# A three-stage convolution kernel: patches in row order, the projection's bias folded into the second group norm, and single matmul blocks between the transposes

## The chip, the cores and the metric

The kernel runs on one core of one Trainium2 chip. The time is the device time of one execution in microseconds (us). A core has TensorE (PE, matmuls and transposes; PEld is its weight load), VectorE (DVE), ScalarE (ACT), GpSimd (POOL), and SyncE (SP), whose queue starts most transfers here. Each engine takes its own instructions in order and waits for the others by semaphores.

## The reference, cut to what matters

The input x has 384 channels of 192 x 192 pixels. Two layers run one behind the other, each behind a group norm over 32 groups:

```python
x = x + conv0(group_norm(x))          # layer 0
x = x + conv1(group_norm(x))          # layer 1

# conv0, its end (channel attention before it, on the image at half size)
out = gelu(attention(q, k, v))                       # (384, 96, 96)
out = repeat(repeat(out, 2, axis=2), 2, axis=3)      # (384, 192, 192)
out = einsum('bchw,oc->bohw', out, w_proj) + b_proj[None, :, None, None]

# conv1: a depthwise 13 x 13, a depthwise 3 x 3 and the identity, each with a batch norm, summed
```

The projection is 1 x 1, so the kernel applies it before the repeat, and each value of the result goes to 2 x 2 pixels.

## The kernel before

Channels lie on partitions, in `CB` = 3 blocks of 128. The stages run one behind the other, with a barrier between them: statistics of x, the QKV stage, the attention matrix, the **Project stage** (`stage_project`), the group norm's constants (`group_affine` with the tag g1), the depthwise kernels (`stage_kernels`), and the **Depthwise stage**.

The Project stage makes the first layer's sum x1 = x + projection and cuts it into patches for the depthwise convolution. It takes 8 image rows (4 at half size) in a step, `STEPS` = 24 steps and a last one that only empties. The work of a step t is written out by hand in `ORDER`, a list that TensorE and ScalarE follow alike:

- **A0 to A2**: TensorE multiplies v by the attention matrix into the bank `pr_ab` (7 matmuls of 384 columns in all, L1019), and ScalarE applies GELU into `ge` (L934).
- **Y0 to Y2**: TensorE projects block n with three matmuls into `pr_yb` (L1028). Then ScalarE adds the bias in place (L937, semaphore `y_ready`), and VectorE adds x (L954, `add`) into the buffer `x1`, writes statistics with `bn_stats` (L959, `record`), and signals `x1_done`.
- **T0 to T11**: the sum of the step before is transposed patch by patch on TensorE (L1005, 39 patches of 128 pixels, up to 4 in a T, two banks `pr_tb`), and ScalarE copies each bank into `turned` (L922). T0 to T3 are block 0, T4 to T7 block 1, T8 to T11 block 2; T3, T7 and T11 hold one patch. A T on TensorE waits until the T two before it is copied (`tr_out`).

A patch is 16 pixels wide and 8 high, shifted by `PAD` = 6 in both directions, so 13 patches (`TJ`) lie across. `x1` holds a patch in column order: `[TJ, TW, TH]`, the row index inside. A step's 8 rows cross the patch edge, so `add` writes 2 rows into the buffer at hand and 6 into the next.

SP stores `turned` to `patch_scratch` for each block (L889, 832 KB) once its four T's are copied, and then loads v (L818, 576 KB) and x (L819, 2304 KB) for the step after next, once `att_done` and `x1_done` of this step are complete. ScalarE's first copy of a block (T0, T4, T8) waits until that block's store of the step before has landed (`stored`).

In the Depthwise stage each partition is one pixel of a patch. TensorE multiplies by a Toeplitz matrix (`cv_toep`) that is loaded for each channel from `toeplitz_scratch` (L1220, 384 KB), row by row in the order of the patch's pixels.

## Time and profile before

| | before |
|---|---|
| time, median of 3 runs | 3220.83 us (3219.31 to 3222.27) |
| time of the profiled execution | 3220.84 us |
| its span in the trace | 3219.1 us |
| PE / DVE / ACT busy over the whole span | 86% / 76% / 43% |
| first matmul of the Project stage | 1747.7 us |
| last copy of the Project stage begins | 2183.65 us |
| first matmul of the Depthwise stage on the chain that ends last | 2252.27 us |

The span runs from the first to the last instruction, and the time lies 1.7 us above it. The chain that ended last is in TensorE for nearly all of the Depthwise stage. The Project stage takes about an eighth of the span.

### The profile page before, as it was taken

How to read it: one execution, taken by the hardware profiler on the slowest of the kernel's cores; microseconds unless marked ns; L12 is line 12 of the kernel's file. 1: busy time of each engine (PE TensorE's matmuls, PEld its weight loads, DVE VectorE, ACT ScalarE, POOL GpSimd, SP SyncE). 2: the span in 40 equal slices, each digit the busy share in tenths (PEclk: the TensorE clock that was granted, in tenths of full speed). 3: DMA queues.
4: the chain of work that ended last, by engine and by line, in shares of the span. 5: the costliest groups of instructions: out<-in, count | busy, mean ns of one | idle time of the engine just before them, and what ended most of it. 6: DMA issues, size and time to landing. Idle time of an engine off the chain costs nothing. (4 is left out here: it accounts for less than half of the span.)

```text
span 3219.1 us, 50624 instructions
## 1 busy us (share of the span) xinstructions
PE 2753.3 (86%) x18393; PEld 2015.4 (63%) x18393; DVE 2458.9 (76%) x3414; ACT 1378.5 (43%) x1771; POOL 22.3 (1%) x39
## 2 busy tenths in 40 slices
PE   0069999999999999999822888884999999999999
PEld 0046566556556556656511555553899999999998
DVE  8934999989989999999894888884566666666663
ACT  0023345445355355353231777773444444444442
POOL 0000000000000000000000000000000000000000
PEclk9999999999999999999956999995999999999999
DMA  9861021111211111111002999986999899999986
GB/s 371 359 224 71 31 81 53 74 55 53 75 53 55 73 54 61 67 45 45 12 18 102 319 322 317 326 278 190 273 283 281 281 280 278 282 280 282 279 257 186
DMA packets 230597, 565.57 MB, mean 176 GB/s; under 512 B 30176, under 2 KB 136256, under 8 KB 227392
## 3 DMA queue, kind: packets, MB, share of 16 engines
q1 hardware_dynamic: 213184, 496.88, 47.6%
q10 hardware_dynamic: 17280, 66.85, 5.4%
q8 instruction: 91, 1.49, 0.2%
q14 instruction: 42, 0.34, 0.0%
HBM read 402.95 MB, written 160.73 MB: 175 GB/s over the span
## 5 line engine op out<-in xcount | busy, mean ns | idle before, releaser
L1380 PE MATMUL cv_cb<-cv_hi,cv_toep 128*128 128x288 f16 (+1 forms) x4608 | 910.9, 290 | 33.5 <-DVE cv_lo L1314 29.7
L650 PE MATMUL qk_qb<-qk_xhi,whi 128*128 128x384 f16 x2592 | 846.2, 326 | 68.6 <-DVE qk_pool L569 41.4
L587 DVE SCALAR_TENSOR_TENSOR qk_dw<-qk_pool,qk_wd,qk_dw 128x768 f32<-128x768 f32 (+1 forms) x936 | 849.9, 957 | 1.4 <-ACT qk_dw L456 1.3
L650 PE MATMUL qk_qb<-qk_xlo,whi 128*128 128x384 f16 x2592 | 845.6, 326 | 0.0
L650 PE MATMUL qk_qb<-qk_xhi,wlo 128*128 128x384 f16 x2592 | 845.5, 326 | 0.0
L1380 PE MATMUL cv_cb<-cv_lo,cv_toep 128*128 128x288 f16 (+1 forms) x2304 | 668.1, 290 | 0.0
L1380 PEld LDWEIGHTS cv_cb<-cv_hi,cv_toep 128*128 128x128 f16 x4608 | 523.3, 114 | 93.8 <-DVE cv_lo L1314 29.8
L569 DVE TENSOR_REDUCE qk_pool<-qk_qb 128x192 f32<-128x768 f32 x432 | 412.5, 955 | 162.5 <-PE qk_qb L650 148.1
L1268 ACT ACTIVATE cv_res<-cv_cb,cv_cst 128x288 f32<-128x288 f32 x384 | 191.8, 501 | 557.5 <-PE cv_cb L1380 557.5
L650 PEld LDWEIGHTS qk_qb<-qk_xhi,whi 128*128 128x128 f16 x2592 | 253.7, 98 | 245.4 <-DVE qk_pool L569 55.6
L1326 DVE COPY cv_rows<-cv_bb 128x512 f32<-128x512 f32 x216 | 146.0, 688 | 323.2 <-PE cv_bb L1361 323.2
L650 PEld LDWEIGHTS qk_qb<-qk_xhi,wlo 128*128 128x128 f16 x2592 | 253.8, 98 | 167.9 <-issue 0.5
L650 PEld LDWEIGHTS qk_qb<-qk_xlo,whi 128*128 128x128 f16 x2592 | 253.8, 98 | 160.8 <-issue 0.3
L466 ACT ACTIVATE qk_pixT<-qk_tb 128x384 f32<-128x384 f32 x146 | 64.4, 488 | 551.3 <-PE qk_tb L619 549.9
L1314 DVE TENSOR_TENSOR cv_lo<-cv_raw,cv_hi 128x1300 f16<-128x1300 f32 x96 | 233.3, 2430 | 61.3 <-ACT cv_hi L1250 61.0
L1380 PEld LDWEIGHTS cv_cb<-cv_lo,cv_toep 128*128 128x128 f16 x2304 | 261.4, 113 | 28.1
L954 DVE TENSOR_TENSOR pr_x<-pr_xb,pr_yb 128x192 f32<-128x192 f32 (+1 forms) x288 | 214.0, 869 | 73.8 <-ACT pr_yb L937 73.8
L922 ACT ACTIVATE pr_turned<-pr_tb 128x512 f32<-128x512 f32 (+1 forms) x300 | 244.2, 923 | 20.7 <-PE pr_tb L1005 19.4
L1250 ACT ACTIVATE cv_hi<-cv_raw 128x1300 f16<-128x1300 f32 x96 | 238.5, 2484 | 27.6 <-DVE cv_raw L1305 27.6
L450 ACT ACTIVATE qk_pool<-qk_pool,qk_bq 128x768 f32<-128x768 f32 x108 | 92.8, 923 | 238.4 <-DVE qk_pool L569 238.4
L1005 PE MATMUL pr_tb<-ident,pr_x 128*128 128x128 f32 x975 | 148.2, 286 | 48.1 <-ACT pr_turned L922 48.1
L1005 PEld LDWEIGHTS pr_tb<-ident,pr_x 128*128 128x128 f32 x975 | 119.0, 145 | 102.8 <-ACT pr_turned L922 63.7
(134 smaller groups left out, 2237.4 us busy)
## 6 DMA issues: line engine op xcount, KB each, us to landing
cv_toep<-toeplitz_scratch SPq DMA_DIRECT2D x384, 384.0 KB, 4.8
patch_scratch<-pr_turned SPq DMA_DIRECT2D x75, 832.0 KB, 7.8
cv_raw<-patch_scratch SPq DMA_DIRECT2D x24, 2600.0 KB, 11.1
st_x<-in_x SPq DMA_DIRECT2D x24, 2304.0 KB, 17.0
qk_xf<-in_x SPq DMA_DIRECT2D x24, 2304.0 KB, 8.1
pr_xb<-in_x SPq DMA_DIRECT2D x24, 2304.0 KB, 9.7
out<-cv_rows ACTq DMA_DIRECT2D x72, 768.0 KB, 5.6
v_scratch<-qk_dw SPq DMA_DIRECT2D x12, 1152.0 KB, 4.4
```

The costliest lines, as they stand in the source:

```text
L450: nc.scalar.activation(pool[:, up, o, 2:2 + UR, 1:1 + PW], pool[:, up, o, 2:2 + UR, 1:1 + PW], ACT.Identity, bias=bq[:, o:o + 1], scale=UN ...
L569: nc.vector.tensor_reduce(pool[:, par, o, 2 + j:4 + j, 1:1 + PW], qbank[g % NQB][:, :, 0:2 * W].rearrange("p j (r x c) -> p j x r c", r=2, ...
L587: nc.vector.scalar_tensor_tensor(acc, pool[:, up, o, y:y + rows_of(u), x:x + PW], wd[:, o, k:k + 1], acc, ALU.mult, ALU.add).then_inc(taps ...
L650: ins = nc.tensor.matmul(qbank[g % NQB][:, h, 0:2 * W], w[:, b, o * P:(o + 1) * P], x[:, half, b, (j + h) * 2 * W:(j + h + 1) * 2 * W], st ...
L922: nc.scalar.activation(turned[:, b, :, j:j + k].rearrange("p c j -> p j c"), tbank[n % 2][:, 0:k * P].rearrange("p (j c) -> p j c", j=k), ...
L954: return nc.vector.tensor_tensor(out.rearrange("p (x c) y -> p y x c", c=2), x, low.unsqueeze(3).broadcast_to([P, n, PW, 2]), ALU.add)
L1005: ins = nc.tensor.transpose(tbank[n % 2][:, j * P:(j + 1) * P], x1[:, par, b, j0 + j].rearrange("p x y -> p (x y)"), ident[:, :])
L1250: nc.scalar.activation(hi[:, par, q * CPP:(q + 1) * CPP, :, 0:TI].rearrange("p c j i -> p (c j) i"), raw[:, par, :, q * CPP:(q + 1) * CPP, ...
L1268: nc.scalar.activation(res[:, par, :, :, c, :], cbank[c % NCB][:, 0:NPIX].rearrange("p (j b i) -> p b j i", b=NBAND, j=OJ), ACT.Identity, ...
L1314: V.tensor_tensor(half, raw[:, par, :, q * CPP:(q + 1) * CPP, :].rearrange("p i c j -> p (c j) i"), hi[:, par, q * CPP:(q + 1) * CPP, :, 0 ...
L1326: V.tensor_copy(dst, src).then_inc(rows_done, 1)
L1380: ins = nc.tensor.matmul(out, toep[:, c % NTOEP, :].rearrange("p (s m v) -> p s v m", s=NS, m=P)[:, s, u * 2 + part], x[:, par, c, u:u + O ...
```

## The change

Four things change.

1. `x1` is `[TJ, TH, TW]`: patches in row order. `add` writes runs of 16 pixels that lie side by side. It has to treat the first patch, the eleven in the middle and the last apart, because of the shift by 6, so that a block takes nine additions in place of four. `record` takes five `bn_stats` in place of three, and `stats1` has 123 records for a channel block in place of 73. The masks of the Depthwise stage and the order in which Toeplitz rows are fetched follow the new pixel order.
2. ScalarE no longer adds the projection's bias. VectorE adds x to the bare projection as soon as `proj_done` says so. `group_affine` adds the bias `bp` to the channels' means (one VectorE instruction, before TensorE's averages), and `stage_kernels` subtracts it from the constant that the Depthwise stage subtracts.
3. `ORDER` has new places: a T stands between A0, A1 and A2, and Y0 to Y8 are single matmuls of the projection (block n // 3, input block n % 3), of which mostly one stands between two T's.
4. GpSimd zeroes the padding with nine instructions in place of three, during the attention stage.

```diff
-    x1 = sb("x1", [P, 2, CB, TJ, TW, TH])
+    x1 = sb("x1", [P, 2, CB, TJ, TH, TW])
...
-        ORDER = ("A0", "A1", "T0", "T1", "A2", "T2", "T3", "T4", "Y0", "T5", "T6", "Y1", "T7", "T8", "Y2", "T9", "T10", "T11")
+        ORDER = ("A0", "T0", "A1", "T1", "A2", "T2", "T3", "Y0", "T4", "Y1", "Y2", "T5", "Y3", "T6", "Y4", "T7",
+                 "Y5", "T8", "Y6", "T9", "Y7", "T10", "Y8", "T11")
...
-                    elif kind == "Y" and (inner or t < STEPS):
-                        act.wait_ge(proj_done, t * CB + n + 1)
-                        nc.scalar.activation(ybank[n][:, 0:PX], ybank[n][:, 0:PX], ACT.Identity,
-                                             bias=bp[:, n:n + 1]).then_inc(y_ready, 1)
...
+                pieces = ((0, 1, PAD, TW, 0), (1, TJ - 1, 0, TW, LEFT), (TJ - 1, TJ, 0, RIGHT, W - RIGHT))
+                low = ybank[b][:, y * PW:(y + n) * PW].rearrange("p (y x) -> p y x", y=n)
+                x = xb[:, par, b, :].rearrange("p (y r x) -> p y r x", r=2, x=W)[:, y:y + n]
+                for j0, j1, x0, x1_, c in pieces:
+                    k, m = j1 - j0, x1_ - x0
+                    lo = low[:, :, c // 2:c // 2 + k * m // 2].rearrange("p y (j x) -> p y j x", j=k)
+                    xs = x[:, :, :, c:c + k * m].rearrange("p y r (j x c) -> p y r j x c", j=k, c=2)
+                    if n == 1:
+                        out = x1[:, buf, b, j0:j1, row:row + 2, x0:x1_].rearrange("p j r (x c) -> p r j x c", c=2)
+                        ins = V.tensor_tensor(out, xs[:, 0], lo.unsqueeze(4).broadcast_to([P, 2, k, m // 2, 2]), ALU.add)
+                        continue
+                    for r in range(2):
+                        out = x1[:, buf, b, j0:j1, row + r:row + r + 2 * n - 1:2, x0:x1_]
+                        ins = V.tensor_tensor(out.rearrange("p j y (x c) -> p y j x c", c=2), xs[:, :, r],
+                                              lo.unsqueeze(4).broadcast_to([P, n, k, m // 2, 2]), ALU.add)
...
-                        dve.wait_ge(y_ready, t * CB + b + 1)
+                        dve.wait_ge(proj_done, t * CB + b + 1)
...
-                        for b in range(CB):
-                            ins = nc.tensor.matmul(ybank[n][:, 0:PX], wp[:, b, n * P:(n + 1) * P], ge[:, b, :],
-                                                   start=b == 0, stop=b == CB - 1)
-                        ins.then_inc(proj_done, 1)
+                        ins = nc.tensor.matmul(ybank[o][:, 0:PX], wp[:, b, o * P:(o + 1) * P], ge[:, b, :],
+                                               start=b == 0, stop=b == CB - 1)
+                        if b == CB - 1:
+                            ins.then_inc(proj_done, 1)
...
+            if offset is not None:
+                V.tensor_tensor(chan[:, :, 0], chan[:, :, 0], offset[:, :], ALU.add).then_inc(chan_ready, 1)
+                dve.wait_ge(chan_ready, CB + 1)
...
-            chained(V.tensor_copy(cst[:, :, 0], mean[:, :]))
+            chained(V.tensor_tensor(cst[:, :, 0], mean[:, :], bp[:, :], ALU.subtract))
...
-                return bass.AP(v.tensor, v.offset, [[JR * TW * NU * 2, TW], [TW * NU * 2, TH], [1, KRUN]])
+                return bass.AP(v.tensor, v.offset, [[TW * NU * 2, TH], [JR * TW * NU * 2, TW], [1, KRUN]])
```

On TensorE, inside the loop of the Project stage, this is the stretch around T4 to T6 before (`pr_tb` is a transposing bank, `pr_yb0` the bank of Y0, `x3` counts equal instructions):

```order
L1024 REGISTER_ALU
L1028 MATMUL pr_yb0<-pr_ge,pr_wp 128x384 [waits pr_x1_done,pr_gelu_done]
L1028 MATMUL pr_yb0<-pr_ge,pr_wp 128x384 x2
L1003 REGISTER_ALU
L1005 MATMUL pr_tb1<-ident,pr_x1 128x128 [waits pr_tr_out]
L1005 MATMUL pr_tb1<-ident,pr_x1 128x128 x3
L1003 REGISTER_ALU
L1005 MATMUL pr_tb0<-ident,pr_x1 128x128 [waits pr_tr_out]
L1005 MATMUL pr_tb0<-ident,pr_x1 128x128 x3
L1028 MATMUL pr_yb1<-pr_ge,pr_wp 128x384 [waits pr_x1_done]
```

The same place now:

```order
L1041 REGISTER_ALU
L1044 MATMUL pr_yb0<-pr_ge,pr_wp 128x384 [waits pr_x1_done,pr_gelu_done]
L1017 REGISTER_ALU
L1019 REGISTER_ALU [waits pr_x1_done]
L1021 MATMUL pr_tb0<-ident,pr_x1 128x128 [waits pr_tr_out]
L1021 MATMUL pr_tb0<-ident,pr_x1 128x128 x3
L1044 MATMUL pr_yb0<-pr_ge,pr_wp 128x384 x2
L1019 REGISTER_ALU
L1021 MATMUL pr_tb1<-ident,pr_x1 128x128 [waits pr_tr_out]
L1021 MATMUL pr_tb1<-ident,pr_x1 128x128 x3
L1044 MATMUL pr_yb1<-pr_ge,pr_wp 128x384 [waits pr_x1_done]
```

The first matmul of the projection now stands ahead of T4 and the other two of its block behind it; between T5 and T6 stands one matmul of the next block, where before T5 and T6 stood together.

On VectorE, this is one block of a step before (`pr_x1` is the sum, `stats1` the records):

```order
L954 TENSOR_TENSOR pr_x1<-pr_xb,pr_yb1 128x192 [waits pr_y_ready]
L954 TENSOR_TENSOR pr_x1<-pr_xb,pr_yb1 128x3x192
L954 TENSOR_TENSOR pr_x1<-pr_xb,pr_yb1 128x192
L954 TENSOR_TENSOR pr_x1<-pr_xb,pr_yb1 128x3x192
L959 ISA [waits pr_x1_done]
L959 BN_STATS stats1<-pr_x1 128x6
L959 ISA
L959 BN_STATS stats1<-pr_x1 128x6
L959 ISA
L959 BN_STATS stats1<-pr_x1 128x6
```

And now, up to the third record:

```order
L963 TENSOR_TENSOR pr_x1<-pr_xb,pr_yb1 128x2x10 [waits pr_proj_done]
L963 TENSOR_TENSOR pr_x1<-pr_xb,pr_yb1 128x2x11x16
L963 TENSOR_TENSOR pr_x1<-pr_xb,pr_yb1 128x2x6
L967 TENSOR_TENSOR pr_x1<-pr_xb,pr_yb1 128x3x10 x2
L967 TENSOR_TENSOR pr_x1<-pr_xb,pr_yb1 128x3x11x16 x2
L967 TENSOR_TENSOR pr_x1<-pr_xb,pr_yb1 128x3x6 x2
L978 ISA [waits pr_x1_done]
L978 BN_STATS stats1<-pr_x1 128x6
L978 ISA
L978 BN_STATS stats1<-pr_x1 128x6
L978 ISA
L978 BN_STATS stats1<-pr_x1 128x6
```

The four additions have become nine, three large and six small, they wait for `proj_done` and not for ScalarE, and two more records follow behind those shown.

On ScalarE, this is the start of a step before (`pr_ge` is GELU's output):

```order
L932 ISA
L933 REGISTER_ALU [waits pr_proj_done]
L934 ACTIVATE pr_ge<-pr_ab0 128x384 [waits pr_att_done]
L933 REGISTER_ALU
L934 ACTIVATE pr_ge<-pr_ab1 128x384 [waits pr_att_done]
L920 REGISTER_ALU
L921 ISA [waits pr_stored0]
L922 ACTIVATE pr_turned<-pr_tb0 128x4x128 [waits pr_tr_done]
```

And now:

```order
L939 ISA
L940 REGISTER_ALU [waits pr_proj_done]
L941 ACTIVATE pr_ge<-pr_ab0 128x384 [waits pr_att_done]
L927 REGISTER_ALU
L928 ISA [waits pr_stored0]
L929 ACTIVATE pr_turned<-pr_tb0 128x4x128 [waits pr_tr_done]
L940 REGISTER_ALU
L941 ACTIVATE pr_ge<-pr_ab1 128x384 [waits pr_att_done]
```

The copy of T0, with its wait for the store of block 0, stood behind the second GELU and now stands ahead of it.

## Rows read from the trace of the kernel before

**Rows 1.** Busy time by stretch: us, then PE, PEld, DVE, ACT, POOL, clock, DMA, GB/s.

```profile
1761.66:2158.90 397.24, 354.33 (x1634) 234.38 (x1633) 331.21 (x484) 284.84 (x415) 0.00 (x0) 1.00 0.94 309
1900.00:2000.00 100.00, 89.20 (x415) 59.03 (x414) 83.75 (x123) 72.15 (x106) 0.00 (x0) 1.00 0.98 322
```

**Rows 2.** Who waited for whom, 1760 to 2160: us, times, longest.

```profile
PEld pr_tb L1005 <- ACT pr_turned L922: 57.0, 91, 1.4
DVE pr_x L954 <- ACT pr_yb L937: 55.2, 23, 5.5
...
PE pr_tb L1005 <- ACT pr_turned L922: 40.5, 49, 1.0
```

**Rows 3.** Timeline of the SP queue, 1940 to 1992: start us, us.

```profile
1942.18 0.40 SPq L818 DMA_DIRECT2D pr_vb<-v_scratch  x1
...
1959.03 0.39 SPq L818 DMA_DIRECT2D pr_vb<-v_scratch  x1
...
1960.50 10.75 SPq L889 DMA_DIRECT2D patch_scratch<-pr_turned  x3
1976.41 0.40 SPq L818 DMA_DIRECT2D pr_vb<-v_scratch  x1
```

**Rows 4.** Timeline of TensorE in one step: start us, us, idle time before it.

```profile
1960.25 0.66 PE L1005 MATMUL pr_tb<-ident,pr_x 128*128 128x128 f32 x4 [0.93 <-ACT pr_turned L922]
...
1962.68 1.04 PE L1005 MATMUL pr_tb<-ident,pr_x 128*128 128x128 f32 x8
1963.55 2.10 PE L1028 MATMUL pr_yb<-pr_ge,pr_wp 128*128 128x384 f32 x6
1965.49 0.71 PE L1005 MATMUL pr_tb<-ident,pr_x 128*128 128x128 f32 x5
```

**Rows 5.** Timeline of ScalarE in the same step.

```profile
1959.15 1.27 ACT L922 ACTIVATE pr_turned<-pr_tb 128x512 f32<-128x512 f32 x2
1960.94 1.05 ACT L922 ACTIVATE pr_turned<-pr_tb 128x512 f32<-128x512 f32 x1 [0.52 <-PE pr_tb L1005]
```

**Rows 6.** Timeline of VectorE in the same step.

```profile
1963.47 2.98 DVE L954 TENSOR_TENSOR pr_x<-pr_xb,pr_yb 128x192 f32<-128x192 f32 x4 [2.55 <-ACT pr_yb L937]
1966.60 1.88 DVE L959 BATCH_NORM_STATS2 stats<-pr_x 128x512 f32 x3
```

**Rows 7.** VectorE groups by shape, whole program: count, busy us, mean ns.

```profile
L1314 DVE TENSOR_TENSOR cv_lo<-cv_raw,cv_hi 128x1300 f16<-128x1300 f32 x96 | 233.3, 2430 | 61.3 <-ACT cv_hi L1250 61.0
L954 DVE TENSOR_TENSOR pr_x<-pr_xb,pr_yb 128x576 f32<-128x576 f32 x144 | 176.9, 1228 | 0.0
...
L552 DVE TENSOR_TENSOR qk_xlo<-qk_xf,qk_xhi 128x1536 f16<-128x1536 f32 x72 | 125.8, 1749 | 15.9 <-ACT qk_xhi L423 15.9
...
L754 DVE TENSOR_TENSOR at_full<-gram,at_colk 96x384 f32<-96x384 f32 x1 | 0.6, 555 | 19.5 <-DMA at_av<-in_a 19.5
```

**Rows 8.** Three half-microsecond stretches of one step: the last two columns are DMA.

```profile
1959.50:1960.00 0.50, 0.00 (x0) 0.00 (x0) 0.50 (x2) 0.50 (x2) 0.00 (x0) 1.00 0.07 22
1964.00:1964.50 0.50, 0.50 (x3) 0.26 (x2) 0.50 (x1) 0.50 (x2) 0.00 (x0) 1.00 1.02 430
1973.00:1973.50 0.50, 0.50 (x5) 0.32 (x4) 0.50 (x2) 0.11 (x1) 0.00 (x0) 1.00 1.10 328
```

**Rows 9.** Stores of L889, 1800 to 2100, issue to landing.

```profile
DMA to landing us min/median/max: 6.0/8.2/12.8
```

**Rows 10.** Timeline behind the Project stage, all engines.

```profile
2189.56 6.11 DVE L147 BATCH_NORM_AGGREGATE g_chan<-stats 128x2 f32<-128x438 f32 x3
```

**Rows 11.** Two short VectorE instructions of the Depthwise stage.

```profile
2228.46 0.32 DVE L1301 TENSOR_SCALAR cv_raw<-cv_raw,cv_side 128x100 f32<-128x100 f32 x1
2228.69 0.30 DVE L1302 TENSOR_SCALAR cv_raw<-cv_raw,cv_side 128x100 f32<-128x100 f32 x1
```

**Rows 12.** Busy time of the Depthwise stage, columns as in the first group.

```profile
2300.00:3150.00 850.00, 850.00 (x6830) 773.04 (x6829) 522.81 (x949) 360.86 (x422) 0.00 (x0) 1.00 0.90 278
```

More of the change, by code:

```diff
@@ L84, in address, with group_affine @@
     return elements
-def group_affine(nc, tag, stats, member, mean, rstd, ahead=None):
+def group_affine(nc, tag, stats, member, mean, rstd, ahead=None, offset=None):
     with ExitStack() as ctx:
@@ L827, in padding @@
     def padding(gp):
[L829 to L833 removed]
+        tail = PAD + W - (TJ - 1) * TW
+        for r in range(2):
+            nc.gpsimd.memset(x1[:, r, :, 0, :, 0:PAD], 0.0).then_inc(zeroed, 1)
+            nc.gpsimd.memset(x1[:, r, :, TJ - 1, :, tail:TW], 0.0).then_inc(zeroed, 1)
+        for b in range(CB):
+            nc.gpsimd.memset(x1[:, 0, b, 1:TJ - 1, 0:PAD, :], 0.0).then_inc(zeroed, 1)
+        nc.gpsimd.memset(x1[:, 0, :, 0, 0:PAD, PAD:TW], 0.0).then_inc(zeroed, 1)
+        nc.gpsimd.memset(x1[:, 0, :, TJ - 1, 0:PAD, 0:tail], 0.0).then_inc(zeroed, 1)
     start = Shared()
[L836 removed]
+    start.vb, start.xb, start.x1, start.wp = vb, xb, x1, wp
     start.c_in, start.zeroed, start.v_in, start.x_in = c_in, zeroed, v_in, x_in
@@ new lines, in add, with record @@
+                return ins
+            def record(n, b, buf, y0, y1):
+                tiles = x1[:, buf, b]
+                rows = y1 - y0
+                per = min(512 // (rows * TW), TJ - 2)
+                for j in range(1, TJ - 1, per):
+                    k = min(per, TJ - 1 - j)
+                    V.bn_stats(stats[:, b, bass.ds(n, 1), :].rearrange("p a s -> p (a s)"),
+                               tiles[:, j:j + k, y0:y1, :].rearrange("p j y x -> p j (y x)"))
+                    n = n + 1
+                V.bn_stats(stats[:, b, bass.ds(n, 1), :].rearrange("p a s -> p (a s)"), tiles[:, 0, y0:y1, PAD:TW])
+                return V.bn_stats(stats[:, b, bass.ds(n + 1, 1), :].rearrange("p a s -> p (a s)"),
+                                  tiles[:, TJ - 1, y0:y1, 0:RIGHT])
@@ L985, in _ @@
             for b in range(CB):
-                flat = x1[:, STEPS % 2, b].rearrange("p j x y -> p (j x) y")[:, PAD:PAD + W, :]
-                for k in range(REC):
-                    ins = record(STEPS * REC - REC + FIRST_REC + k, b, flat[:, k * W // REC:(k + 1) * W // REC, 0:PAD])
+                ins = record(STEPS * REC - REC + FIRST_REC, b, STEPS % 2, 0, PAD)
             ins.then_inc(st_done, 1)
@@ L1171, in sem @@
             return ctx.enter_context(nc.semaphore(f"cv_{name}"))
-        raw, side, rowsel, raw_in, masked = start.raw, start.side, start.rowsel, start.raw_in, start.masked
+        raw, side, colsel, raw_in, masked = start.raw, start.side, start.colsel, start.raw_in, start.masked
         hi = sb("hi", [P, 2, GRP, TJ, TIP], F16)
```

85 lines of the change are left out of this document (35 added, 50 removed).

## The prediction

> **What bounds the kernel now.** I read first the busy time by stretch. The 23 steps of the Project stage's loop, from the first matmul of step 1 to the last step's end, take 397.24 us, so 17.27 us a step; TensorE is busy for 354 of them, VectorE for 331, ScalarE for 285 [rows 1]. No engine is full, and the transfers have a share of 0.94 to 0.98 at 309 to 322 GB/s [rows 1]. The next view, who waited for whom, shows two couplings: TensorE waits for ScalarE's copies of the transposes 57.0 us as weight load and 40.5 us as matmul (the same gaps seen twice in part), and VectorE waits 55.2 us in 23 waits for the bias pass [rows 2]. The start times of the v load give the step: 16.85 us, then 17.38 us [rows 3]. They alternate, since the loop holds two steps, so the loop's own branch and registers cost some 0.5 us in two steps.
>
> The other place the change touches is the Depthwise stage. There TensorE is busy 850.00 of 850 us [rows 12]: only a later start or a starved TensorE would move it. So the time falls or rises by what the Project stage does, plus what lies between the stages.
>
> **TensorE in a step.** The timeline gives the rate of issue, free of the overlap of durations. Eight transposes take from 1962.68 to 1963.55, 0.109 us each; one block of three projection matmuls (six rows in the trace, each matmul is two) takes from 1963.55 to 1965.49, so 0.323 us a row [rows 4]. A step has 39 transposes, 18 rows of projection and 14 of attention: 39 x 0.109 + 32 x 0.323 = 14.6 us. The rest, 2.3 to 2.7 us, is waiting, 0.93 us of it at T4 for the copy of T2 [rows 4] and most of the rest where T8 to T11 follow each other: a copy starts 0.69 us after its T (1960.25 to 1960.94), and takes 1.05 us alone [rows 4, 5], against 0.44 us of transposes.
>
> The new order puts 0.65 us of projection between T's: a pair takes 0.44 + 0.65 = 1.09 us, as long as a copy. I walked through the new order with these numbers. A0, T0, A1, T1, A2, T2, T3 take 5.95 us. Y0 must wait for the third GELU, 0.2 us. T2's copy then stands behind that GELU and ends at about 7.2, so that T4 waits 0.4 us. Behind T4 nothing waits. The sum is 15.3 us; with half of the loop's 0.5 us, **15.5 us**.
>
> **VectorE in a step.** A block costs now 2.98 us of additions and 1.88 us of statistics [rows 6], 14.6 us a step. The 576 elements of the large addition take 1228 ns [rows 7], 1.87 ns each once a fixed 0.15 us is taken off. Two kinds of row bracket the new form, for the trace of before has none of it: 1300 elements of which one input is read at a stride took 2430 ns, 1.75 each; 1536 elements that lie side by side took 1749 ns, 1.04 each beside 0.15 us, and 384 read from a bank of PSUM took 555 ns, 1.04 too [rows 7]. The new addition writes runs of 16 side by side, reads x side by side and the bank as before. I take 1.04, since what is left of the old form, a bank of PSUM read beside SBUF, is the fast row; the other end, 1.87, stays in the range. The Trainium skill speaks of the same thing ("SBUF — State Buffer", section on the DMA port swizzle): SBUF answers at full rate when at least two accesses in a row fall into one line of 16 bytes. By that rule the old write, 32 bytes apart, paid, and the new one would not; the slow strided row agrees, and no row here isolates the write.
>
> More instructions cost their start. Of a back-to-back pair the second begins 0.23 us after the first, of which 100 strided elements are 0.19 [rows 11]: 0.05 us. Additions: 1536 x 1.04 + 9 x 0.06 = 2.1 us. Statistics: 1.88 + 2 x 0.08 = 2.0 to 2.1 us. A block takes 4.2 us, a step **12.7 us**. VectorE then waits for TensorE, and this covers any error up to 2.5 us a step; beyond it VectorE is the bound.
>
> Against this stands a rule of the Trainium skill ("VectorE: DVE Perf Modes", the section on the TRN2 errata): each instruction pays its fixed cost, about 151 cycles, anew. What the rows show instead is an overlap: the three statistics of 512 elements took 1.88 us together [rows 6]. By that page's figure at its 0.96 GHz, an estimate, 42 instructions of a step would cost 6.6 us beside 9216 elements at 1.04 ns, 16.2 us in all; the rows' way gives 12.7.
>
> **ScalarE.** Three bias passes of 0.56 us go; nothing is added. Its copies set the pace of the T's but leave it idle otherwise.
>
> **The transfers.** A step moves 576 KB of v, 2304 KB of x and three stores of 832 KB. In half-microsecond stretches x comes at 430 GB/s and stores go at 328 to 333 [rows 8]: 5.5 us and 7.7 us; v at the rates between them is 1.4 to 1.8 us. That is 14.7 to 15.0 us. The second bound: 200 such stretches from 1900 to 2000 fall short of a full share by 8.4 us together (the gap behind 1959.5 is one, 22 GB/s [rows 8]), so that in 17.13 us, the mean of two steps, the transfers work 15.6 us. Both include no gap. So **14.7 to 15.6 us** is a second floor beside TensorE's 15.5.
>
> It is coupled by the stores. A store of block 0 goes behind the x load: from issue to landing up to 12.8 us [rows 9]. Issued at 1960.50 [rows 3], it lands at about 1972.8, and T0's copy follows at 1973.8. In the new kernel x1 of block 2 is complete some 4.4 us into the next step, the load is issued then, and block 0's store at about 7.4, when T3 is copied. The load ends at 12, the store at 15 and lands at 16.5; T0's copy wants it at 15.5 + 2.0 = 17.5. That fits by 1 us, not more. If it is late, both later GELUs are queued behind T0's copy on ScalarE, TensorE waits at Y0, and VectorE and the next load come later. I therefore take not 15.6 but **15.9 us** a step.
>
> **Between the stages.** VectorE's three `bn_aggr` over 438 values took 6.11 us [rows 10]; TensorE's averages wait for them. 738 values are 6.11 x 738/438 = 10.3 us, **+4.2 us**, in full on the path. The addition of the bias to the means is +0.2 us, the new subtraction replaces a copy. The emptying of the last 78 transposes is set by ScalarE's copies, as before. GpSimd's nine memsets run in the attention stage, 40 us before anyone needs them. The first matmuls of step 0 are unchanged.
>
> **The sum.** 23 x (17.27 - 15.9) = 31.5 us less, 4.4 us more: 27.1 us. The profiled execution took 3220.84 us, the median is 3220.83, so no correction is due: **3194 us** (-0.8%).
>
> **The rivals.**
> - *The forecast*, a step of 15.5 to 16.5 us: 3185 to 3208. Chance 0.66.
> - *Every VectorE instruction pays its start in full*, nothing overlaps any longer when instructions are short. The fixed 0.15 us [rows 7] for each of 42 instructions: 9.6 + 6.3 = 15.9, with the gaps at semaphores 16.4 us a step: 3221 - 20 + 4.4 = 3205. Against it: the overlap in [rows 6, 11]. Chance 0.08. (This is what the rule of "VectorE: DVE Perf Modes" in the Trainium skill comes to.)
> - *The transfers do not close up.* The share of 0.98 [rows 1] may mean that they work at their limit, and what looks like a gap is the start of a load. Then a step stays at 16.9, and T0's copy waits for the store where T4 waited before: 23 x 0.35 = 8 less, 4.4 more, 3217. For it: the landing of 12.8 us. Against it: from 1959.5 on hardly anything flows, 22 GB/s [rows 8]. Chance 0.10.
> - *VectorE becomes the bound* (the other side): the additions stay at 1.87 ns an element, because it was the doubled reading of PSUM that was slow. Then a block has 2.9 us of elements, nine starts, and 2.1 us of statistics: 5.5 us with 0.06 us a start, 5.8 with the starts of small ones at 0.1 us more, 16.5 to 17.5 a step, and with gaps and the loop 16.9 to 17.9. It is slower than before from a step of 17.1 on; the price is up to 23 x 0.6 + 4.4 = 18 us: 3217 to 3239, in the middle 3228. Chance 0.10, a third of it within 0.2%.
> - *The Depthwise stage starves.* The Toeplitz rows are fetched in another order, neighbours 3968 bytes apart in place of 128. The transfers' share there is 0.90 at 278 GB/s [rows 12], and 55% of the bytes are Toeplitz rows. The point from which it decides is a fetch 18% longer; at 25% longer the share would be 1.04, and 4% of 960 us are 36 us: 3230. The same bytes and the same lengths speak against it. Chance 0.06.
>
> **How the numbers follow.** A measurement of this kernel tells some 0.2%, 6.4 us, from no change. Faster by more: the forecast and the second, with a bit of the third, 0.76. Within: most of the third and a third of the fourth, 0.12. Slower: the rest, 0.12. The forecast alone has the range 3185 to 3208; to leave out no more than 2 in 10 it reaches up over the second and third rivals, and down to a step of 15.3: 3181 to 3220.
>
> **What would show it.** The v load's start times 15.5 to 16.3 us apart; the large addition (528 elements) at about 0.70 us, where 1.14 us would prove the fourth rival; no bias pass, and VectorE waiting for `pr_yb` on TensorE at each block; T4 the only T that waits, and T0's copy beginning on a landing in some steps; `bn_aggr` at 3.4 us each; Toeplitz fetches landing in 4.8 us as before. I am wrong if waits for the store of block 0 fill every step, if VectorE has no idle time, or if TensorE has any in the Depthwise stage.

## The result: 7.3% slower, and where the time went

The changed kernel took **3456.76 us** (3452.48 to 3462.03, four runs) against 3221.39 (3219.31 to 3222.27, four runs): a ratio of 1.0732, interval 1.0714 to 1.0751. The forecast was 3194, its range 3181 to 3220. Its profiled execution took 3462.03 us, with a span of 3460.3.

One row splits the span in two: the load of the constants, with which SP enters the Depthwise stage. First the kernel before, then the one after (timeline of SP, start us, us):

```profile
2222.44 0.34 SPq L1205 DMA_DIRECT2D cv_cst<-constant_scratch  x1
```

```profile
2199.26 0.34 SPq L1222 DMA_DIRECT2D cv_cst<-constant_scratch  x1
```

Up to there the change won 23.2 us. From there to the end of the span the kernel before needs 3219.1 - 2222.4 = 996.7 us, and the one after 3460.3 - 2199.3 = 1261.0: 264.4 us lost. 264.4 - 23.2 = 241.2, the difference of the spans. So there are two separate questions: did the Project stage do what was forecast, and what happened to the Depthwise stage?

**The Depthwise stage.** Busy time by stretch of the kernel after, columns as in [rows 1]:

```profile
1900.00:2000.00 100.00, 95.68 (x440) 59.64 (x439) 77.86 (x258) 68.84 (x93) 0.00 (x0) 1.00 1.04 339
2300.00:3150.00 850.00, 691.24 (x5202) 597.71 (x5201) 399.30 (x726) 275.42 (x321) 0.00 (x0) 0.91 0.69 214
```

Where TensorE was full for 850 of 850 us [rows 12] it is now busy for 691, at a granted clock of 0.91; the share of the transfers fell from 0.90 to 0.69 and their rate from 278 to 214 GB/s. The first reading is misleading: it looks as if the transfers had become idle. The waits of 2250 to 3400 name them as what is waited for:

```profile
PE cv_cb L1397 <- DMA cv_toep<-toeplitz_scratch: 199.3, 47, 9.8
```

The page of the kernel after gives the packets and the fetches (for which it prints no landing time any more; it was 4.8 us):

```profile
DMA packets 227525, 565.56 MB, mean 163 GB/s; under 512 B 27104, under 2 KB 133184, under 8 KB 224320
...
cv_toep<-toeplitz_scratch SPq DMA_DIRECT2D x384, 384.0 KB
```

There are 3072 fewer small packets (under 512 B) than the 30176 of the kernel before: 8 fewer for each of the 384 fetches. SP, which issues the fetches, is at times held up in the issue itself. Its timeline, and behind it the line of the fetch from 2300 to 3150 (duration of one in ns: least, median, longest):

```profile
2575.49 48.88 SPq L1237 DMA_DIRECT2D cv_toep<-toeplitz_scratch  x15
2624.59 1.84 SPq L1143 DMA_DIRECT2D cv_raw<-patch_scratch  x1
2626.63 54.07 SPq L1237 DMA_DIRECT2D cv_toep<-toeplitz_scratch  x16
```

```profile
L1237 SPq DMA_DIRECT2D cv_toep<-toeplitz_scratch x258: 616/621/13452, 2298.6 to 3148.9; - x129
```

The 48.88 us reach from the start of the first of fifteen fetches to the end of the last and hold SP's waits for free buffers too; in the kernel before, fifteen reach over 36.31. Summed one by one, the fifteen issues themselves take 29.3 us in place of 8.1. From 2300 to 3150, 89 of 257 issues take more than 1 us, and the longest 13.45; before, none of 337 took more than 0.60.

On TensorE one such place reads so (start us, us, idle time before it); the matmuls behind the wait start 0.24 us apart:

```profile
2591.94 0.29 PE L1397 MATMUL cv_cb<-cv_hi,cv_toep 128*128 128x276 f16 x1
2592.06 0.60 PE L1378 MATMUL cv_bb<-ident,cv_res 128*128 128x128 f32 x4
2601.80 0.43 PE L1397 MATMUL cv_cb<-cv_hi,cv_toep 128*128 128x288 f16 x1 [9.14 <-DMA cv_toep<-toeplitz_scratch]
2602.03 0.44 PE L1397 MATMUL cv_cb<-cv_lo,cv_toep 128*128 128x288 f16 x1
2602.27 0.68 PE L1397 MATMUL cv_cb<-cv_hi,cv_toep 128*128 128x288 f16 x2
...
2605.91 0.29 PE L1397 MATMUL cv_cb<-cv_hi,cv_toep 128*128 128x288 f16 x1
2606.03 0.29 PE L1397 MATMUL cv_cb<-cv_lo,cv_toep 128*128 128x288 f16 x1
2606.16 0.41 PE L1397 MATMUL cv_cb<-cv_hi,cv_toep 128*128 128x288 f16 x2
```

From 2605 on it is 0.12 us. The granted clock of these two stretches, and of the wait ahead of them:

```profile
2592.70:2601.70 9.00, 0.00 (x0) 0.00 (x0) 5.30 (x10) 0.17 (x1) 0.00 (x0) 0.79 0.57 220
2601.80:2604.40 2.60, 2.60 (x11) 1.58 (x12) 0.00 (x0) 0.00 (x0) 0.00 (x0) 0.50 0.51 197
2605.00:2610.00 5.00, 5.00 (x43) 4.59 (x41) 1.39 (x2) 3.27 (x3) 0.00 (x0) 1.00 0.46 119
```

TensorE waits 9.14 us for the fetch, and then runs its next matmuls at the lower of its two levels (0.50 is 1.2 GHz of 2.4). So a stall costs more than itself. An estimate for the whole stretch from 2300 to 3150: 5202 records of matmuls, where the kernel before has 6830 in 850 us [rows 12], would take 647 us at its pace; TensorE was busy for 691. Of the 203 us lost there, 159 are idle time and 44 a slower clock.

**The Project stage.** Start times of the loads on SP, 1925 to 1976, for [rows 3]:

```profile
1925.35 0.39 SPq L820 DMA_DIRECT2D pr_vb<-v_scratch  x1
...
1941.40 0.40 SPq L820 DMA_DIRECT2D pr_vb<-v_scratch  x1
...
1957.70 0.39 SPq L820 DMA_DIRECT2D pr_vb<-v_scratch  x1
...
1974.07 0.39 SPq L820 DMA_DIRECT2D pr_vb<-v_scratch  x1
```

The v loads stand 16.05, 16.30 and 16.37 us apart. From the third of the stage (1767.93) to the last (2105.27) lie 21 steps, 16.06 us each; before they were 17.22 (1768.64 to 2130.30). The mean hides a drift: the first three steps take 15.48, 15.48 and 15.19 us, the last ten 16.3 to 16.5. The waits there, 1760 to 2130, for [rows 2]:

```profile
DVE pr_x L963 <- PE pr_yb L1044: 71.2, 23, 4.1
PEld pr_tb L1021 <- ACT pr_turned L929: 49.9, 83, 1.0
...
ACT pr_turned L929 <- DMA patch_scratch<-pr_turned: 41.0, 18, 2.9
```

VectorE waits for TensorE, as forecast, and has idle time (busy for 77.86 of the 100 us above). ScalarE's copies wait 18 times for a store, 2.3 us each. One block of VectorE, for [rows 6]:

```profile
1934.70 0.67 DVE L963 TENSOR_TENSOR pr_x<-pr_xb,pr_yb 128x20 f32<-128x20 f32 x3
1935.29 1.67 DVE L967 TENSOR_TENSOR pr_x<-pr_xb,pr_yb 128x30 f32<-128x30 f32 x6
1937.10 1.75 DVE L978 BATCH_NORM_STATS2 stats<-pr_x 128x512 f32 x3
1938.76 0.23 DVE L981 BATCH_NORM_STATS2 stats<-pr_x 128x80 f32 x1
1938.91 0.19 DVE L982 BATCH_NORM_STATS2 stats<-pr_x 128x48 f32 x1
1939.02 0.67 DVE L963 TENSOR_TENSOR pr_x<-pr_xb,pr_yb 128x20 f32<-128x20 f32 x3
```

It takes from 1934.70 to 1939.02, 4.32 us, although the additions are nine and the records five. The large addition and the most frequent small one, and the aggregation behind the stage:

```profile
L967 DVE TENSOR_TENSOR pr_x<-pr_xb,pr_yb 128x528 f32<-128x528 f32 x144 | 94.3, 695 | 0.0
...
L967 DVE TENSOR_TENSOR pr_x<-pr_xb,pr_yb 128x30 f32<-128x30 f32 x144 | 19.6, 177 | 0.0
```

```profile
2161.80 10.18 DVE L147 BATCH_NORM_AGGREGATE g_chan<-stats 128x2 f32<-128x738 f32 x3
```

The large addition is (695 - 150) / 528 = 1.03 ns an element. The small ones last 177 ns, but overlap: the nine start and end within some 2.3 us. The aggregation takes 10.18 us, 4.07 more than in [rows 10].

### The profile page after: what moved, and what is told of

Same layout as the page of the kernel before. It is cut to its first block and busy times, and to the rows that moved or that the text cites. A ratio compares the mean times of both kernels' runs of the same rounds, so it can differ in the third digit from the quotient of the medians.

```text
span 3460.3 us, 51200 instructions
## 1 busy us (share of the span) xinstructions
PE 2810.3 (81%) x18393; PEld 2012.8 (58%) x18393; DVE 2422.3 (70%) x3925; ACT 1351.8 (39%) x1699; POOL 22.3 (1%) x45
## 5 line engine op out<-in xcount | busy, mean ns | idle before, releaser
L1397 PE MATMUL cv_cb<-cv_hi,cv_toep 128*128 128x288 f16 (+1 forms) x4608 | 951.3, 298 | 240.1 <-DMA cv_toep<-toeplitz_scratch 201.4
L1397 PEld LDWEIGHTS cv_cb<-cv_hi,cv_toep 128*128 128x128 f16 x4608 | 531.2, 115 | 337.2 <-issue 205.9
L1397 PE MATMUL cv_cb<-cv_lo,cv_toep 128*128 128x288 f16 (+1 forms) x2304 | 686.6, 298 | 0.0
L929 ACT ACTIVATE pr_turned<-pr_tb 128x512 f32<-128x512 f32 (+1 forms) x300 | 254.6, 907 | 95.8 <-PE pr_tb L1021 54.4
L1397 PEld LDWEIGHTS cv_cb<-cv_lo,cv_toep 128*128 128x128 f16 x2304 | 266.7, 116 | 36.5
L1021 PE MATMUL pr_tb<-ident,pr_x 128*128 128x128 f32 x975 | 159.5, 279 | 22.9 <-ACT pr_turned L929 21.5
L1044 PE MATMUL pr_yb<-pr_ge,pr_wp 128*128 128x384 f32 x432 | 171.2, 493 | 0.7 <-ACT pr_ge L941 0.6
## 6 DMA issues: line engine op xcount, KB each, us to landing
cv_raw<-patch_scratch SPq DMA_DIRECT2D x24, 2600.0 KB, 26.4
pr_xb<-in_x SPq DMA_DIRECT2D x24, 2304.0 KB, 12.6
```

The costliest lines, as they stand in the source:

```text
L929: nc.scalar.activation(turned[:, b, :, j:j + k].rearrange("p c j -> p j c"), tbank[n % 2][:, 0:k * P].rearrange("p (j c) -> p j c", j=k), ...
L1021: ins = nc.tensor.transpose(tbank[n % 2][:, j * P:(j + 1) * P], x1[:, par, b, j0 + j].rearrange("p y x -> p (y x)"), ident[:, :])
L1044: ins = nc.tensor.matmul(ybank[o][:, 0:PX], wp[:, b, o * P:(o + 1) * P], ge[:, b, :], start=b == 0, stop=b == CB - 1)
L1397: ins = nc.tensor.matmul(out, toep[:, c % NTOEP, :].rearrange("p (s m v) -> p s v m", s=NS, m=P)[:, s, u * 2 + part], x[:, par, c, u:u + O ...
```

## The experiments

The theory behind the first four: a Toeplitz fetch is spread over as many DMA engines as its outermost dimension allows. Before, that dimension has `TW` = 16 steps of 8 rows; after, `TH` = 8 steps of 16 rows. With 8, only half of the 16 engines carry it. The rival is the order of addresses, neighbours 3968 bytes apart. The change moved both at once. In the first four and in the one with four steps the order of the Toeplitz rows does not fit that of the patches, so only their time has a meaning, not their output.

**The old fetch in the kernel after.**

```diff
-                return bass.AP(v.tensor, v.offset, [[TW * NU * 2, TH], [JR * TW * NU * 2, TW], [1, KRUN]])
+                return bass.AP(v.tensor, v.offset, [[JR * TW * NU * 2, TW], [TW * NU * 2, TH], [1, KRUN]])
```

> The changed kernel with one line undone: the Toeplitz rows are fetched in the old order (outermost 16 steps of 3968 bytes, in each 8 steps of 128 bytes). The patches stay in row order, so the Toeplitz rows no longer belong to the pixels of their partitions; all instructions and bytes are the same. If the fetch's pattern alone costs the 236 us (either of the two theories below), the Depthwise stage is TensorE-bound again, 40.3 us a group, and since the changed kernel started that stage 23 us earlier than the kernel before, the time is 3221 - 23 = 3198 us (3190 to 3206). If the loss comes from elsewhere in the change (masks, patches), it stays above 3400.

Measured: 3200.87 us, ratio 0.9943 (0.9926 to 0.996). TensorE is full again, 500.00 of 500 us from 2500 to 3000, and from the constants' load to the end it takes 996.0 us, as before. One line of the diff holds all of the loss, and the time is inside the range expected.

**The new fetch in the kernel before**, the same edit the other way round.

> The kernel before with only the new pattern of the Toeplitz fetch: outermost 8 steps of 128 bytes, in each 16 steps of 3968 bytes. It fetches rows to other partitions than the patches' pixels. If the fetch's pattern alone costs the time: 3221 + 259 = 3480 us (3460 to 3500), since the changed kernel lost 235 us net of the 23 us that its Project stage gave. If it needs the rest of the change: 3221.

Measured: 3479.31 us, ratio 1.0806 (1.0785 to 1.0828). That is 259.6 us above its kernel before (3219.73); with the 18.9 us of the first experiment, the two parts give 3221.39 + 259.6 - 18.9 = 3462.1, and the change as a whole 3456.76. They add to within 5.3 us.

**Addresses and outermost count apart**, both in the kernel before. First far addresses with 16 outermost steps, then near addresses with 8:

```diff
-                return bass.AP(v.tensor, v.offset, [[JR * TW * NU * 2, TW], [TW * NU * 2, TH], [1, KRUN]])
+                return bass.AP(v.tensor, v.offset, [[TW * NU * 2, 2 * TH], [JR * TW * NU * 2, TW // 2], [1, KRUN]])
```

```diff
-                return bass.AP(v.tensor, v.offset, [[JR * TW * NU * 2, TW], [TW * NU * 2, TH], [1, KRUN]])
+                return bass.AP(v.tensor, v.offset, [[2 * JR * TW * NU * 2, TW // 2], [TW * NU * 2, 2 * TH], [1, KRUN]])
```

> The kernel before with a fetch of outermost 16 steps of 128 bytes, in each 8 steps of 3968 bytes: the same 128 runs of 3072 bytes in size and number, neighbours 3968 bytes apart as in the changed kernel, but 16 steps outermost as before. The values fetched are partly others. Theory 'count of the outermost dimension' (8 outermost steps spread a transfer over 8 of the 16 DMA engines): 3221 us. Theory 'address order' (neighbouring runs far apart are slow): 3440 or more.

> The kernel before with a fetch of outermost 8 steps of 7936 bytes, in each 16 steps of 128 bytes: neighbours 128 bytes apart as before, but 8 steps outermost as in the changed kernel. The values fetched are partly others. Theory 'count of the outermost dimension': about 3480 us, and each fetch has 8 packets fewer (3072 in all). Theory 'address order': 3221 us.

Measured: far addresses with 16 steps 3220.49 us, ratio 1.0001 (0.9991 to 1.0012); near addresses with 8 steps 3463.36 us, ratio 1.0757 (1.0735 to 1.0778). Busy time of the two from 2500 to 3000:

```profile
2500.00:3000.00 500.00, 500.00 (x4019) 454.75 (x4018) 307.96 (x559) 212.77 (x248) 0.00 (x0) 1.00 0.91 280
```

```profile
2500.00:3000.00 500.00, 406.31 (x3066) 352.89 (x3065) 238.18 (x426) 162.95 (x190) 0.00 (x0) 0.90 0.68 216
```

and their packets, on their pages:

```profile
DMA packets 230597, 565.57 MB, mean 176 GB/s; under 512 B 30176, under 2 KB 136256, under 8 KB 227392
```

```profile
DMA packets 227525, 565.56 MB, mean 163 GB/s; under 512 B 27104, under 2 KB 133184, under 8 KB 224320
```

The small packets follow the outermost count, and so does nearly all of the time. With 16 steps far addresses cost nothing. With 8 they cost something: far ones (3479.31) take 16 us more than near ones (3463.36), against 244 us for the count alone.

Those DMA engines can be seen at work. The traces hold a record of each packet, without the number of its engine. Counted over ten groups of 16 channels, from the first load of `cv_raw` behind 2500 on, the number of packets under way at the same moment is this (the mean time is that of a packet of 3072 bytes, the fetch's own; landing updates are those of the semaphores on which TensorE waits for fetches):

| outermost steps | most frequent number under way | share of the time at it | 15 or more under way | mean time of a fetch's packet | landing updates, one fetch |
|---|---|---|---|---|---|
| 16 (before) | 16 | 50% | 78% | 184 ns | 16 |
| 16, far (`far16`) | 16 | 50% | 77% | 184 ns | 16 |
| 8, near (`near8`) | 8 | 44% | 35% | 149 ns | 9 |
| 8, far (after) | 8 | 45% | 35% | 154 ns | 9 |
| 4, near (`near4`, below) | 4 | 64% | 22% | 133 ns | 5 |

In the wait of 9.14 us shown above (2592.7 to 2601.7) eight are under way for 69% of the time. So a fetch occupies as many engines as its outermost dimension has steps. The Trainium skill has the rule in "DMA: Bandwidth & Descriptors", in the section on why a DMA increments its semaphore by 16: a transfer gets the largest number of engines, up to 16, that divides the size of the slowest dimension larger than one in both access patterns. The traces agree, by this table and by the 8 small packets fewer for a fetch of 8 steps.

**Four outermost steps**, to ask for the size of the effect. Groups of 16 channels start 40.33 us apart in the kernel before (the loads of `cv_raw`) at a share of 0.90 [rows 12], so all 16 engines work 36.3 us in each. If T of this is Toeplitz fetches and O the rest, the busy half works 2T + O with 8 steps; near8's groups are 52.3 us apart, and those of the kernel after 52.9, which makes T 16 to 17.

```diff
-                return bass.AP(v.tensor, v.offset, [[JR * TW * NU * 2, TW], [TW * NU * 2, TH], [1, KRUN]])
+                return bass.AP(v.tensor, v.offset, [[4 * JR * TW * NU * 2, TW // 4], [TW * NU * 2, 4 * TH], [1, KRUN]])
```

> near8 with 4 outermost steps of 15872 bytes, in each 32 steps of 128 bytes; the values fetched are partly others. The model: a transfer is spread over as many DMA engines as the outermost dimension has steps, so the busiest engines have T x 16/k of Toeplitz work and O of everything else for each group of 16 channels. From the kernel before, 0.90 of 40.3 us: T + O = 36.3. From near8, 52.3 us a group at a mean share of 0.68 and full busiest engines: 2T + O = 52.3 and T + O = 35.6, so T = 16.7 and O = 18.9 us. With k = 4 a group takes 4T + O = 85.7 us, 33.4 more than in near8, and 23 to 24 groups of it give 3463 + 785 = 4248 us (4150 to 4350), at a mean share of 36/86 = 0.42. Theory 'any count under 16 takes one slower path of the queue': like near8, 3460 to 3500 us.

Measured: 4100.03 us in one run (before 3219.38). Stretch and packets:

```profile
2500.00:3000.00 500.00, 316.90 (x2077) 243.30 (x2075) 161.84 (x286) 110.92 (x128) 0.00 (x0) 0.87 0.44 145
```

```profile
DMA packets 225989, 565.55 MB, mean 138 GB/s; under 512 B 25568, under 2 KB 131648, under 8 KB 222784
```

Again 4608 / 384 = 12 small packets fewer for each fetch: 16, 8, 4. The direction holds and a single slower path is out, but the size was expected too large: groups are 77.8 us apart (17 groups, 2562.74 to 3884.68). From 8 to 4 steps they grow by 25.5 us, which makes 2T = 25.5 and T = 12.7. From 16 to 8 the same model would give 36.3 + 12.7 = 49.0 us for the 52.3 measured.

The model takes a packet's time as fixed, and the table above shows that it is not. A group has 2048 packets of 3072 bytes. At 184 ns they are 23.6 us of work on each of 16 engines (not 16 to 17), at 149 ns 38.1 us on each of 8, at 133 ns 67.8 us on each of 4. The other transfers, spread over all 16, go from 13.1 us to 16.8 and 17.3. The sums for the engines that carry fetches, 54.9 and 85.1 us, lie above the groups' 52.3 and 77.8, since packets overlap in part: nine, or five, are under way for a tenth of the time. So a fetch's packets get shorter the fewer engines carry them, and the others' longer; why stays open.

**Row order kept, the fetch repaired.** The kernel after with the old fetch and the old masks; the patches are brought into column order when they are loaded, by the order of the partitions' rows:

```diff
+        v = patch_dram[:, bass.ds(g, 1), :, :].rearrange("p a i n -> p (a i n)")
+        row = NG * TI * GRP * TJ
         sp.dma_start(raw[:, par].rearrange("p i c j -> p (i c j)"),
-                     patch_dram[:, bass.ds(g, 1), :, :].rearrange("p a i n -> p (a i n)")).then_inc(raw_in[par], 16)
+                     bass.AP(v.tensor, v.offset, [[row, TW], [TW * row, TH], [1, TI * GRP * TJ]])).then_inc(raw_in[par], 16)
```

> The changed kernel with the pixel order mended elsewhere: the patches are stored in row order, but the Depthwise stage loads them in column order (the load's outermost dimension is 16 columns, in each 8 rows, whole rows of 20.8 KB), so that the Toeplitz rows can be fetched in the old way, 16 steps outermost; the masks are those of before. The output is the reference's. If the count of the outermost dimension is the whole cause, TensorE is full again in the Depthwise stage and the time is that of e1: 3201 us (3194 to 3206), 0.6% under the kernel before. If the load of patches suffers from the new order, it lands later than 11 us and the time is higher.

Measured: 3205.76 us (3197.29 to 3208.44), ratio 0.9954 (0.994 to 0.9968). The step is 16.17 us. The Depthwise stage takes 3204.8 - 2199.3 = 1005.5 us, 9 more than before. The patches' loads have this row on its page, 17.0 us to landing where the kernel before has 11.1 and the first experiment 10.8:

```profile
cv_raw<-patch_scratch SPq DMA_DIRECT2D x24, 2600.0 KB, 17.0
```

From 2500 on TensorE is full (650.00 of 650 us); the 9 us lie at the start, where nothing is ahead. It is full without reserve: a packet of this load (20800 bytes) takes 1533 ns in place of 852, the transfers' share from 2500 to 3150 is 1.00 in place of 0.90, and the Toeplitz fetches land after 9.8 us in place of 4.8. This kernel, called the base from here on, is what four of the next six edit, for the Project stage.

**The order undone.** Y in blocks of three matmuls again, every other part of the change kept:

```diff
-        ORDER = ("A0", "T0", "A1", "T1", "A2", "T2", "T3", "Y0", "T4", "Y1", "Y2", "T5", "Y3", "T6", "Y4", "T7",
-                 "Y5", "T8", "Y6", "T9", "Y7", "T10", "Y8", "T11")
+        ORDER = ("A0", "A1", "T0", "T1", "A2", "T2", "T3", "T4", "Y0", "Y1", "Y2", "T5", "T6", "Y3", "Y4", "Y5",
+                 "T7", "T8", "Y6", "Y7", "Y8", "T9", "T10", "T11")
```

> fix_x_outer with the order of before: the three matmuls of a block of the projection stand together, and T4 ahead of Y0, T5 and T6 behind each other. Theory 'transfers bound the step' (a step of 16.2 us since T0's copy waits for the store of block 0): TensorE's waits come back in part (T4, T8 to T11), a step of 16.3 to 16.6, 3203 to 3210 us. Theory 'the order is what the Project stage gained from': a step of 16.9, 3215 to 3220 us.

Measured: 3230.15 us, ratio 1.0037 (1.0025 to 1.0049): slower than before, and above both ranges. Steps of 17.00 us, and TensorE busy for

```profile
1900.00:2000.00 100.00, 89.41 (x420) 59.44 (x418) 73.38 (x247) 64.56 (x88) 0.00 (x0) 1.00 0.98 324
```

Without the order a step is only 0.22 us shorter than before, so the second theory, 16.9, is the nearer one; the time is higher still since aggregation (4.1 us) and the start of the Depthwise stage are paid all the same. TensorE's waits for ScalarE's copies are back: 42.6 us as weight load and 32.1 as matmul from 1760 to 2100. The 24.4 us between this kernel and its base are more than the base's whole gain of 13.6 us. VectorE is idle for 27 of 100 us, and that does not help.

**ScalarE's pass brought back**, as a copy in place with its semaphore; VectorE waits for it again:

```diff
+                    elif kind == "Y" and n % CB == CB - 1 and (inner or t < STEPS):
+                        o = n // CB
+                        act.wait_ge(proj_done, t * CB + o + 1)
+                        nc.scalar.activation(ybank[o][:, 0:PX], ybank[o][:, 0:PX], ACT.Copy).then_inc(y_ready, 1)
...
-                        dve.wait_ge(proj_done, t * CB + b + 1)
+                        dve.wait_ge(y_ready, t * CB + b + 1)
```

> fix_x_outer with ScalarE's pass over the projection put back, as a plain copy in place (the bias stays folded), and VectorE waiting for it. ScalarE is busy for 11.3 us of 16.2, three passes of 0.56 us fit in. Theory 'transfers bound the step': VectorE and the next load start 0.6 us later, which shifts the store of block 0 as well, 3201 to 3206 us. If ScalarE is near its limit between T5 and T11 (copy 1.0 us for each 1.09 us), each pass delays a T by 0.3 to 0.5 us: 3210 to 3220.

Measured: 3198.21 us, but spread from 3188.92 to 3214.05 over five runs, ratio 0.9944 (0.9922 to 0.9966), overlapping with its base; the median is below both expectations. In the profiled execution, the fastest, a step took 15.39 us. No cost of the pass shows; whether its delay helps, by letting stores land ahead of loads, is left open.

**Patches in column order**, the kernel before with the new `ORDER`, its single matmuls and the folded bias, and nothing else:

> The kernel before with the new order and the folded bias, but patches in column order: four additions and three records a block, the slow additions of 1.23 us, 73 records for bn_aggr in place of 123. VectorE needs 14.6 us a step, under the 16.2 us of the changed kernel. Theory 'transfers bound the step': x1 of block 2 is complete some 2.2 us later in the step, so the load, the store of block 0 and T0's copy are later too: a step of 16.3 to 16.9, less 4.2 us for bn_aggr: 3198 to 3212 us. Theory 'VectorE's faster additions are what gained': a step of 17 and more, 3212 to 3220.

Measured: 3191.73 us (3188.41 to 3196.28), ratio 0.9917 (0.9902 to 0.9932), 14.0 us less than the repaired kernel in row order. Stretch and waits:

```profile
1900.00:2000.00 100.00, 97.67 (x452) 61.55 (x453) 90.02 (x132) 71.29 (x95) 0.00 (x0) 1.00 1.04 349
```

```profile
ACT pr_turned L925 <- DMA patch_scratch<-pr_turned: 47.7, 22, 4.2
...
DVE pr_x L952 <- PE pr_yb L1026: 45.0, 24, 18.1
```

The step is 16.00 us with the old, slow additions; VectorE is 90% busy and does not set the pace. Both theories expected more (from 16.3 and from 17). Between the two profiled executions the difference is 15.1 us: 4.1 of aggregation, 8.0 of the Depthwise stage (997.5 against 1005.5), and 3 in the Project stage.

**Two buffers for what a store holds.** In the base, and in the kernels with the new order so far, a copy waits for a store. `turned` gets a second buffer and each buffer its own semaphores, in the repaired kernel:

```diff
-        turned = sb("turned", [P, CB, P, TJ])
+        turned = sb("turned", [P, 2, CB, P, TJ])
...
-        stored = [sem(f"stored{b}") for b in range(CB)]
+        stored = [[sem(f"stored{q}_{b}") for b in range(CB)] for q in range(2)]
```

> fix_x_outer with two buffers turned in turn (a semaphore for each): T0's copy waits for the store of the step before last, which landed long ago. In fix_x_outer T0's copy waits for block 0's store in 18 of 22 steps, 2 to 3 us each. Theory 'ring of waits' (T0's copy, the GELUs behind it, the projection, x1, the load, the store behind the load): the wait goes and TensorE sets the step, 15.3 us by the walk, 22 x 0.9 = 20 us less than fix_x_outer, 3185 us (3180 to 3190). Theory 'transfers are at their limit' (16.2 us of work in a step): the wait moves to x or v, the step stays at 16.2: 3203 to 3207.

Measured: 3190.73 us (3189.47 to 3193.88), ratio 0.9915 (0.9902 to 0.9928). Its step is 15.31 us (1765.66 to 2087.21, 21 steps), and

```profile
1900.00:2000.00 100.00, 99.12 (x465) 63.39 (x463) 81.37 (x273) 75.34 (x98) 0.00 (x0) 1.00 1.07 362
```

TensorE is 99% busy. The step is that of the theory of the ring, the time 0.7 us above its range. The same transfers that had a share of 1.04 at 339 GB/s now have 1.07 at 362.

**The load behind the store**, the other way to cut that wait: in the repaired kernel SP issues v and x of the next step behind the store of block 0.

```diff
-                if inner or t + 2 < STEPS:
...
-                    sp.wait_ge(att_done, t * CB + CB)
-                    sp.wait_ge(x1_done, t * CB + CB)
-                    start.load(sp, t + 2, par)
+                        if b == 0 and (inner or t + 1 < STEPS):
...
+                            sp.wait_ge(att_done, t * CB)
+                            sp.wait_ge(x1_done, t * CB)
+                            start.load(sp, t + 1, 1 - par)
```

> fix_x_outer with SP's queue in another order: the load for step t + 1 is issued in step t behind the store of block 0, instead of the load for t + 2 at the end of step t, ahead of it. The same bytes, one buffer of turned. Theory 'ring of waits': block 0's store no longer queues behind 2.9 MB, it lands some 5 us after its issue and T0 doesn't wait: 15.3 us a step, 3185 us (3180 to 3192). Theory 'transfers are at their limit': 3203 to 3207, with waits for other stores or for x.

Measured: 3206.14 us, ratio 0.9957 (0.9944 to 0.997); one execution of six took 6249.91 us, is not in the ratio, and stays unexplained. Nothing was won. The waits show why, and ScalarE's timeline says where:

```profile
ACT pr_turned L929 <- DMA patch_scratch<-pr_turned: 39.7, 20, 2.7
```

```profile
1908.21 1.28 ACT L929 ACTIVATE pr_turned<-pr_tb 128x512 f32<-128x512 f32 x2
1912.19 3.09 ACT L929 ACTIVATE pr_turned<-pr_tb 128x512 f32<-128x512 f32 x4 [2.70 <-DMA patch_scratch<-pr_turned]
```

The wait has about the sum that it has in the kernel after (41.0). T0 and T1 (the first row) no longer wait; the copy of T4 does, 2.70 us, for the store of block 1. The number is the one that the theory of the limit gave, but that theory is refuted by the experiment before, where the same transfers ran in steps of 15.31 us: here the wait moved to the next store.

**Both best parts together**, column order with two buffers:

> u3_column_order (patches in column order, new order, folded bias) with two buffers turned. Its steps last 15.35 and 16.3 us in turn, and T0's copy waits 47.7 us in 22 waits. Theory 'ring of waits': 15.3 us in each, less than u3_column_order by 11 x 0.9 = 10 us: 3181 us (3177 to 3186), 4 us under fix2_two_turned, since bn_aggr has 73 records a block and not 123. VectorE works 14.6 us of 15.3; if its semaphore gaps fill the rest it is the bound, and the step is 15.5 to 15.8: 3186 to 3192.

Measured: **3174.42 us** (3170.16 to 3176.15), ratio 0.9858 (0.9843 to 0.9872), the fastest of all and below the range of its first theory. Steps of 15.41 us, VectorE 93% busy:

```profile
1900.00:2000.00 100.00, 98.53 (x456) 62.32 (x455) 92.79 (x136) 75.31 (x98) 0.00 (x0) 1.00 1.06 355
```

## Why the prediction was wrong, point by point

- **The step that failed** is the rival "The Depthwise stage starves", and in it the sentence "The same bytes and the same lengths speak against it". It priced the fetch by bytes, lengths and distance of addresses, and gave 0.06 to 3230 us; the sum itself put the stage at no change. Bytes and lengths are the same, and distance costs nothing with 16 steps (3220.49). What changed is the number of engines that carry a fetch: 8 in place of 16. The prediction's own last sign of being wrong, idle time of TensorE in the Depthwise stage, is what came.
- **What the rows held.** At a share of 0.90 on all 16 engines, 40.33 us of a group hold 36.3 us of work on each [rows 12]. An estimate with the prediction's 55% of the bytes as share of the time: fetches 20.0 us and the rest 16.3, so the half that carries fetches works 2 x 20.0 + 16.3 = 56.3 us. Measured are groups of 52.9 us (12 groups, 2516.84 to 3152.01). The work as a whole has not changed: 0.69 of 52.9 us are 36.5. A lower mean share is here the same work in a longer time, with half of the engines idle in part of it.
- **The rival's own sums** were off as well. To fill the groups a fetch had to be (40.33 / 36.3 - 1) / 0.55 = 20% longer, not 18%, and one 25% longer makes a share of 0.90 x (1 + 0.55 x 0.25) = 1.02, not 1.04. Neither matters beside the 264 us lost where the rival had 36.
- **The Project stage's steps held.** Forecast 15.9 us a step, measured 16.06; aggregation +4.2, measured +4.07; up to the constants' load 27.1 us were forecast and 23.2 came. With the old fetch put back the rest of the change measures 3200.87, and the repaired kernel 3205.76, both inside the range; the term 23 x (17.27 - 15.9) = 31.5 was 26.7 (23 x 1.16).
- **TensorE's walk**, 15.3 us: the kernel after has it in its first steps only (15.48, 15.48, 15.19), with two buffers it is the mean (15.31).
- **VectorE**: 1.04 ns an element taken, 1.03 measured; 4.2 us a block, 4.32 measured. The rivals of full starts and of VectorE as the bound are out. Three blocks take 13.0 us, where the rule of the Trainium skill in "VectorE: DVE Perf Modes" (section on the TRN2 errata) gave an estimate of 16.2: the trace does not agree, since back-to-back instructions overlap. The additions sped up in the direction of the Trainium skill's rule in "SBUF — State Buffer" (section on the DMA port swizzle); but the order of x and the split of the instructions changed with the write, and no run isolates it.
- **But VectorE's speed was not where the gain came from.** The prediction charged everything to a sum in which VectorE is covered, and so did not say which part earns the time. The single matmuls between the T's earn it (24.4 us with the rest kept). Column order, with additions of 1.2 us, has a step of 16.00; with two buffers it has 15.41 where row order has 15.31. So the faster additions are worth 0.1 us a step with two buffers and nothing that shows without, and the layout that allows them costs 12 us behind the stage, 8 of them by the reordered load of the repair.
- **The ring of the store of block 0**: "That fits by 1 us, not more." It did not fit: T0's copy waits for the store, 41.0 us in 18 waits. The term that was too small is the store's own time: 9.1 us from issue to landing (7.4 to 16.5), where the stores issued at 1944.85 and 1961.22 took 12.4 and 12.6. One step of the kernel after, on ScalarE:

```profile
1941.03 1.05 ACT L929 ACTIVATE pr_turned<-pr_tb 128x512 f32<-128x512 f32 x1 [2.46 <-DMA patch_scratch<-pr_turned]
```

  The 0.4 us allowed for the ring were 0.75 (16.06 against 15.31). That the step came out near 15.9 is partly luck: the walk with its loop was 0.2 us too long, the ring 0.35 too short.
- **The transfers' floor**, 14.7 to 15.6 us: the upper end was too high, since a step of 15.31 ran. A share of 1.04 was no limit; 1.07 ran.
